# A selective scan's backward direction: two of its sixteen input products move to ScalarE and TensorE

## The chip, the cores and the metric

The kernel runs on one core of one Trainium2 chip. The metric is the device time of one execution in microseconds (us). Lower is better.

## The reference, cut to what matters

The whole network is an attention layer, a recurrent layer, a Mamba layer and a mixture of experts over 16384 tokens of 64 channels. The change touches the Mamba layer alone, which runs once over the tokens as they stand and once over them reversed:

```python
dt = jax.nn.softplus(dt @ dt_w.T + dt_b)
A = -jnp.exp(A_log)
dA = jnp.exp(dt[..., None] * A)
dBx = dt[..., None] * Bm[:, :, None, :] * xc[..., None]

def step(h, inp):
    dA_t, dBx_t, C_t = inp
    h = dA_t * h + dBx_t
    y = jnp.einsum('bds,bs->bd', h, C_t)
    return (h, y)
...
y = jnp.swapaxes(ys, 0, 1) + xc * D
y = y * jax.nn.silu(z)
return y @ out_w.T
...
y_bwd = jnp.flip(_mamba(jnp.flip(x_flat, axis=1), *params), axis=1)
return (y_fwd + y_bwd).reshape(Bn, Hn, Wn, C)
```

There are 128 inner channels and 16 states. `xc` is the SiLU of a causal convolution with four taps; `Bm`, `Cm` and the raw `dt` are linear in `xc`.

## The kernel before, in words

Stages run one after the other on all engines: attention, recurrence, normalization, the scan (`state_scan`), experts. The scan keeps the 128 inner channels on the partitions and takes the tokens in 16 blocks of 1024 for each direction, `NC = 16`, forward first. Inside a block it takes the 16 states in turn, s = 0 to 15; below, such a turn is called unit s.

For each state and block the following happens, each on a tile of 128 x 1024:

- **The decay**, exp(dt A[s]), is made by ScalarE: into the SBUF ring `dA` (`decay_v`) or into the PSUM buffer `p_u[s % 2]` (`decay_g`).
- **The input product**, dt x times B's row s, comes about in one of three ways. *By VectorE* (`BY_VECTOR`): TensorE spreads B's row over all partitions into `p_u[s % 2]` (`spread_b` of TensorE) and VectorE multiplies in place (`inject` of VectorE); the decay is then in SBUF. *By GpSimd* (the states in neither table): SP loads the row spread over all partitions, 512 KB, into the ring `bb`, and GpSimd multiplies into `dbx` (`inject` of GpSimd); the decay is then in `p_u[s % 2]`. *By ScalarE and TensorE's turns* (`BY_SCALAR`): dt x stands transposed in `dtxT`, tokens on the partitions, so that B is a scale per partition; ScalarE makes eight scaled copies of 128 x 128 (`scale`), and TensorE turns these back into `p_u[s % 2]` (`turn_in`); the decay is in SBUF.
- **The scan**, by VectorE (`tensor_tensor_scan`, in `unit`), reads decay and input and writes the ring `h`.
- **The read**, by GpSimd (`read_c`), multiplies `h` by C's row into the ring `hc`, and TensorE adds it up over the states in `p_y` (`total`), four units later (`LAG_SUM`).

Before, the forward direction has eight states by VectorE, four by ScalarE (3, 5, 9, 12) and four by GpSimd; backward has ten by VectorE, none by ScalarE and six by GpSimd (2, 5, 7, 10, 13, 15).

While a block is scanned, the next one is prepared through one PSUM buffer, `p_p`, which passes from step to step: the convolution (TensorE, units 0 and 1), its SiLU (`silu_x`, ScalarE, unit 1), the rows of B and C (`in_out`, TensorE, units 2 and 3), their copy and store (`bc_rows`, ScalarE, unit 4), backward the gate's input (`gate_in`, unit 4, and `take_z`, unit 5), the step size (`step_size`, unit 6), its softplus (ScalarE, VectorE and GpSimd's `linear_and_log`, units 7 to 11) and dt x (`dt_x`, VectorE, unit 12). Where states go by ScalarE, B's columns (`columns_b`, `take_columns_b`) and the turned dt x (`turn_x`, `take_turned_x`) pass through it too. Backward, the block before is finished as well: the gate (VectorE, behind unit 3's scan), which waits for the last of the 16 sums, the projection (`project`, TensorE) and its addition to `x` (`add_x`, VectorE).

The order is written out by hand. `run` calls each engine's `unit` for s = 0 to 15 and behind it the steps that the engine's tables `prepare`, `tail` and `own` name for this s. Every engine works strictly in its order and waits on semaphores. In `unit`, each engine works ahead by a number of states:

```python
C_RING, B_RING, TURN_RING = 4, 2, 2
DECAY_AHEAD, INJECT_AHEAD, SCALE_AHEAD, LAG_SUM = 3, 2, 3, 4
```

So ScalarE issues state 4's decay and scalings in unit 1, and TensorE issues state 4's spreading or turn in unit 3, ahead of the sum that is due in that unit. A `p_u` buffer comes free for state s when the scan of state s - 2 is done.

## Time and profile before

| | |
|---|---|
| median of 3 runs | 2569.32 us (2566.36 to 2575.73) |
| the profiled execution | 2567.49 us, span 2565.7 us |
| busy: TensorE, VectorE, ScalarE, GpSimd | 2189.9, 2180.1, 1763.6, 2076.0 us |
| forward scan | about 650 to 1488 us |
| backward scan | about 1488 to 2363 us |

Busy times are sums of instruction durations. TensorE's are partly modelled, and neighbouring instructions of VectorE, ScalarE and GpSimd overlap by up to 0.1 us, so that the start-to-start distance in the timeline is the better measure of what one costs. "Idle before" names who ended an engine's idle time.

### The profile page before, as it was taken

The page shows a single profiled execution, that of the slowest core. Times are in us where ns is not written, and L with a number is a line of the kernel's source. Part 1 is how long each engine was busy: PE and PEld are TensorE (multiplying, and loading weights), DVE is VectorE, ACT ScalarE, POOL GpSimd, SP SyncE. Part 2 cuts the span into 40 slices and gives each one's busy share as a digit, 9 for nine tenths or more (in the row PEclk, how much of TensorE's full clock was granted, in tenths as well). Part 3 has the DMA queues.
Part 4 walks back from the last instruction along what each step waited for, and adds up shares of the span by engine and source line. Part 5 has one row for each costly group of instructions (what it writes and reads, how often), then busy time and mean ns, then how long its engine had stood idle before and what let it go on. Part 6 is the DMA issues. An engine that isn't in the chain of part 4 may idle for free. (4 is left out here: it accounts for less than half of the span.)

```text
span 2565.7 us, 37339 instructions
## 1 busy us (share of the span) xinstructions
PE 2189.9 (85%) x9229; PEld 1137.4 (44%) x9306; DVE 2180.1 (85%) x2229; ACT 1763.6 (69%) x3998; POOL 2076.0 (81%) x1330
## 2 busy tenths in 40 slices
PE   8899997774799888998899888899889898887597
PEld 8566665562344444444444433343333333333543
DVE  5577777434899999999999999999999999997766
ACT  4799997565788877887788855656556565553386
POOL 4355555203899999999999999999999999997389
PEclk7899998786899999999999999999999999999799
DMA  3000000003677676676667777777777777773032
GB/s 70 13 12 12 12 11 9 1 1 85 222 228 231 219 232 225 231 230 226 227 226 235 228 240 253 244 231 239 239 234 248 233 244 237 230 245 127 3 69 60
DMA packets 192553, 421.10 MB, mean 164 GB/s; under 512 B 66548, under 2 KB 95705, under 8 KB 192474
## 3 DMA queue, kind: packets, MB, share of 16 engines
q1 hardware_dynamic: 190938, 416.01, 51.6%
q10 hardware_dynamic: 1536, 4.20, 0.5%
q8 instruction: 30, 0.49, 0.1%
q14 instruction: 49, 0.40, 0.1%
HBM read 387.63 MB, written 24.12 MB: 160 GB/s over the span
## 5 line engine op out<-in xcount | busy, mean ns | idle before, releaser
L1574 POOL TENSOR_TENSOR s_hc<-s_h,s_cc 128x1024 f32<-128x1024 f32 x512 | 1202.6, 2370 | 51.0 <-PE s_py L1337 37.3
L1337 PE MATMUL s_py<-s_hc,ident 128*128 128x512 f32 x2048 | 979.3, 603 | 19.1 <-DVE s_yo L1620 19.1
L1657 DVE TENSOR_TENSOR_SCAN s_h<-s_dA,s_state,s_pu 128x1024 f32<-128x1024 f32 x330 | 770.3, 2342 | 27.7 <-PE s_pu L1315 4.7
L1337 PEld LDWEIGHTS s_py<-s_hc,ident 128*128 128x128 f32 x2048 | 385.9, 193 | 384.7 <-issue 312.0
L1490 ACT ACTIVATE s_dA<-s_dt,ss_A 128x1024 f32<-128x1024 f32 x352 | 401.6, 1142 | 9.1 <-ACT s_brow L1453 7.7
L1495 ACT ACTIVATE s_pu<-s_dt,ss_A 128x1024 f32<-128x1024 f32 x160 | 178.4, 1115 | 322.0 <-DVE s_h L1657 316.8
L1567 POOL TENSOR_TENSOR s_dbx<-s_dtx,s_bb 128x1024 f32<-128x1024 f32 x160 | 379.1, 2369 | 6.9 <-DMA s_bb<-rows_scratch 6.9
L1657 DVE TENSOR_TENSOR_SCAN s_h<-s_pu,s_state,s_dbx 128x1024 f32<-128x1024 f32 x150 | 350.2, 2335 | 22.3 <-ACT s_pu L1495 20.1
L1633 DVE TENSOR_TENSOR s_pu<-s_pu,s_dtx 128x1024 f32<-128x1024 f32 x288 | 349.0, 1212 | 14.9 <-PE s_pu L1324 12.5
L1324 PE MATMUL s_pu<-s_bcs,ss_sel 128*128 128x512 bf16 x499 | 159.6, 390 | 133.8 <-DVE s_h L1657 129.7
L591 POOL TENSOR_TENSOR ar_ex<-ar_ex,ar_rs 128x512 f32<-128x512 f32 x128 | 133.3, 1041 | 157.8 <-DVE ar_rs L540 157.7
L629 ACT ACTIVATE ar_ex<-ar_sc,ar_mn 128x128 f32<-128x128 f32 x512 | 199.2, 391 | 5.5 <-DVE ar_mn L535 3.0
L1324 PEld LDWEIGHTS s_pu<-s_bcs,ss_sel 128*128 128x128 bf16 x576 | 42.1, 98 | 323.6 <-DVE s_h L1657 224.5
L1473 ACT ACTIVATE s_sT<-s_dtxT,s_bT 128x128 f32<-128x128 f32 x512 | 156.4, 388 | 0.2
L1925 PE MATMUL ee_ps<-ex_we,ex_xg 128*128 128x512 f32 x256 | 113.9, 606 | 30.2 <-DMA ex_xg<-ex_xT 30.2
L1270 PE MATMUL s_pp<-s_n,ss_taps 128*128 128x512 f32 x256 | 122.3, 601 | 10.3 <-DMA s_n<-n_scratch 10.3
L531 DVE TENSOR_TENSOR ar_sc<-ar_pss,at_bias 128x512 f32<-128x512 f32 x128 | 88.6, 692 | 18.3 <-PE ar_pss L475 15.5
L1943 ACT ACTIVATE ee_hw<-ee_ps,ex_wt 128x64 f32<-128x64 f32 x384 | 92.2, 317 | 15.7 <-PE ee_ps L1925 6.4
L1982 POOL TENSOR_TENSOR ee_hw<-ee_hw 128x1024 f32<-128x1024 f32 x32 | 75.4, 2355 | 33.6 <-DVE ee_hw L1951 33.6
L553 DVE SCALAR_TENSOR_TENSOR x_tok<-ar_pso,at_maskT,x_tok 128x64 f32 (+1 forms) x128 | 36.2, 283 | 76.8 <-POOL x_tok L586 70.7
L1502 ACT COPY s_state<-s_h 128x1 f32<-128x1 f32 x510 | 86.9, 180 | 18.5 <-DVE s_h L1657 17.9
L629 ACT ACTIVATION_READ_ACCUMULATOR ar_ex<-ar_sc,ar_mn 128x1 f32 x512 | 96.3, 188 | 0.0
(272 smaller groups left out, 3590.3 us busy)
## 6 DMA issues: line engine op xcount, KB each, us to landing
s_cc<-rows_scratch SPq DMA_DIRECT2D x512, 512.0 KB, 4.6
s_bb<-rows_scratch SPq DMA_DIRECT2D x160, 512.0 KB, 5.0
s_n<-n_scratch SPq DMA_DIRECT2D x64, 258.0 KB, 5.5
y_scratch<-s_yo SPq DMA_DIRECT2D x16, 512.0 KB, 5.4
s_yf<-y_scratch SPq DMA_DIRECT2D x16, 512.0 KB, 6.6
x_tok<-in_x_dram SPq DMA_DIRECT2D x16, 256.0 KB, 4.5
at_xg<-at_xT SPq DMA_DIRECT2D x64, 64.0 KB, 2.1
n_scratch<-ss_turned SPq DMA_DIRECT2D x32, 128.0 KB, 2.8
```

The source lines that it names most:

```text
L591: nc.gpsimd.tensor_tensor(ex[:, j, :, :], ex[:, j, :, :], by_head, ALU.mult).then_inc(evened, 1)
L629: ins = nc.scalar.activation(ex[:, j, h, :], sc[:, j, h, :], ACT.Exp, bias=mn[:, j, h:h + 1], scale=-1.0, accum_out=tot[:, j, h:h + 1])
L1270: ins = nc.tensor.matmul(p_p[:, hf], lhsT=k["taps"][:, int(w.back), pair, :], rhs=ns[:, par, at:at + HALF], start=(pair == 0), stop=(pair ...
L1324: ins = nc.tensor.matmul(p_u[s % 2][:, hf], lhsT=k["sel"][:, s:s + 1].to_broadcast([128, 128]), rhs=bcs[:, par, hf], start=True, stop=True)
L1337: ins = nc.tensor.matmul(p_y[:, hf], lhsT=c.ident[:, :], rhs=hc[:, s % RING, hf], start=(s == 0), stop=(s == U - 1))
L1473: ins = nc.scalar.activation(sT[:, r % TURN_RING, j, :], dtxT[:, j, :], ACT.Copy, scale=bT[:, par, j, s:s + 1])
L1490: nc.scalar.activation(dA[:, w.d.index(s) % w.decay_ring, :], dt[:, par, :], ACT.Exp, scale=k["A"][:, s:s + 1]).then_inc(v_decayed, 1)
L1495: nc.scalar.activation(p_u[s % 2][:, :], dt[:, par, :], ACT.Exp, scale=k["A"][:, s:s + 1]).then_inc(g_decayed, 1)
L1567: nc.gpsimd.tensor_tensor(dbx[:, r % B_RING, :], dtx[:, par, :], bb[:, r % B_RING, :], ALU.mult).then_inc(g_injected, 1)
L1574: nc.gpsimd.tensor_tensor(hc[:, s % RING, :], h[:, s % RING, :], cc[:, s % C_RING, :], ALU.mult).then_inc(read, 1)
L1633: nc.vector.tensor_tensor(p_u[s % 2][:, :], p_u[s % 2][:, :], dtx[:, par, :], ALU.mult).then_inc(v_injected, 1)
L1657: nc.vector.tensor_tensor_scan(out=flow(h[:, s % RING, :]), data0=flow(decays), data1=flow(inputs), initial=begun, op0=ALU.mult, op1=ALU.a ...
```

## The change

Backward, states 4 and 10 go by ScalarE and TensorE's turns, nine states (0, 1, 3, 6, 7, 9, 12, 13, 15) by VectorE and five (2, 5, 8, 11, 14) by GpSimd. Backward blocks therefore also make B's columns (unit 5 on TensorE, 6 on ScalarE) and the turned dt x (units 13 and 14). The projection moves from unit 13 to unit 14 and waits for the turned dt x to be copied, its addition from unit 14 to 15. The step size waits for the copied columns, the columns wait for the copied gate input. The ring of decays has four buffers (five before). The waits on B's ring count for five products in two slots: `spreads` counts the loads of one slot, and SP's `spread_b` waits, at the first rows of a block, for the last user of that slot in the block before. Forward blocks are as before.

```diff
 BY_VECTOR = ((0, 1, 4, 7, 8, 11, 13, 15),
-             (0, 1, 3, 4, 6, 8, 9, 11, 12, 14))
-BY_SCALAR = ((3, 5, 9, 12), ())
+             (0, 1, 3, 6, 7, 9, 12, 13, 15))
+BY_SCALAR = ((3, 5, 9, 12), (4, 10))
...
-        self.decay_ring = 4 if len(self.d) % 4 == 0 else 5
+        self.decay_ring = 5 if len(self.d) % 5 == 0 else 4
...
+    def spreads(self, n, slot):
+
+        w = self.of(n)
+        per = len(range(slot, len(w.g), B_RING))
+        done = NC * len(range(slot, len(w.before.g), B_RING)) if w.before is not None else 0
+        return n * per + (done - w.start * per)
...
             def step_size(hf):
                 def step(w, m, par):
-                    bc_taken(w, m)
-                    if w.back:
-                        need(pe, z_copied, m - NC)
+                    pe.wait_ge(bt_taken, m + 1)
...
             def columns_b(w, m, par):
                 pe.wait_ge(r_copied, m + 1)
+                if w.back:
+                    need(pe, z_copied, m - NC)
...
             def project(w, m, par):
-                pe.wait_ge(dtx_done, end(m + 3, ALL))
+                pe.wait_ge(xt_taken, end(m + 3, ALL))
...
-                backward: shared + [(5, step_size(a)), (6, step_size(b))]}
-            tail = {forward: (), backward: [(13, project)]}
+                backward: shared + [(5, columns_b), (6, step_size(a)), (6, step_size(b)), (13, turn_x)]}
+            tail = {forward: (), backward: [(14, project)]}
...
-                       backward: first + rest_of}
+                       backward: first + [(6, take_columns_b)] + rest_of + [(14, take_turned_x)]}
...
-            tail = {forward: (), backward: [(LAG_SUM - 1, gate), (14, add_x)]}
+            tail = {forward: (), backward: [(LAG_SUM - 1, gate), (15, add_x)]}
...
                 r = w.g.index(s)
                 if r == 0:
                     sp.wait_ge(r_stored, 16 * (n + 1))
-                need(sp, g_injected, w.upto(G, n) + r + 1 - B_RING)
+                if r >= B_RING:
+                    sp.wait_ge(g_injected, w.upto(G, n) + r - B_RING + 1)
+                elif n:
+                    last = range(r, len(way_of(n - 1).g), B_RING)[-1]
+                    sp.wait_ge(g_injected, w.upto(G, n) - len(way_of(n - 1).g) + last + 1)
```

Three places of the order follow, each in a late backward block. Line numbers are those of either kernel; behind the first tables they differ by one.

**ScalarE, units 1 to 4**, from the decay of state 4 (the first `s_dA`) on; `s_state` is the copy of a scan's last column, `s_brow` that of the rows of B and C. Before:

```order
L1490 ACTIVATE s_dA<-s_dt,ss_A 128x1024
L1502 COPY s_state<-s_h 128x1
L1409 ACT_TABLE_LOAD
L1409 ACTIVATE s_xc<-s_pp,ss_cb 128x1024
L1415 ACTIVATE s_zs<-s_zs 128x1024
L1418 ACT_TABLE_LOAD
L1502 COPY s_state<-s_h 128x1
L1490 ACTIVATE s_dA<-s_dt,ss_A 128x1024
L1502 COPY s_state<-s_h 128x1
L1495 ACTIVATE s_pu<-s_dt,ss_A 128x1024
L1502 COPY s_state<-s_h 128x1
L1453 COPY s_brow<-s_pp 32x1024
```

Now, from the same decay:

```order
L1489 ACTIVATE s_dA<-s_dt,ss_A 128x1024
L1501 COPY s_state<-s_h 128x1
L1472 ACTIVATE s_sT<-s_dtxT,s_bT 128x128 x8
L1408 ACT_TABLE_LOAD
L1408 ACTIVATE s_xc<-s_pp,ss_cb 128x1024
L1414 ACTIVATE s_zs<-s_zs 128x1024
L1417 ACT_TABLE_LOAD
L1501 COPY s_state<-s_h 128x1
L1489 ACTIVATE s_dA<-s_dt,ss_A 128x1024
L1501 COPY s_state<-s_h 128x1
L1494 ACTIVATE s_pu<-s_dt,ss_A 128x1024
L1489 ACTIVATE s_dA<-s_dt,ss_A 128x1024
```

The eight scalings of state 4 stand between its decay and the table load of the convolution's SiLU (`s_xc`), and the decay of state 7, the last row, is ahead of the copy of the rows, which follows it.

**TensorE, units 1 to 5**, from the second half of the convolution (`ss_taps`) on; `s_py` are the sums, `s_pu` from `s_bcs` a spreading, `ss_wbc` into 32 rows the rows of B and C, `ss_wz` the gate's input. Before:

```order
L1270 MATMUL s_pp<-s_n,ss_taps 128x512 x2
L1324 MATMUL s_pu<-s_bcs,ss_sel 128x512 x2
L1337 MATMUL s_py<-s_hc,ident 128x512 x2
L1289 MATMUL s_pp<-s_xc,ss_wbc 32x512
L1324 MATMUL s_pu<-s_bcs,ss_sel 128x512 x2
L1337 MATMUL s_py<-s_hc,ident 128x512 x2
L1289 MATMUL s_pp<-s_xc,ss_wbc 32x512
L1337 MATMUL s_py<-s_hc,ident 128x512 x2
L1253 MATMUL s_pp<-s_n,ss_wz 128x512 x2
L1324 MATMUL s_pu<-s_bcs,ss_sel 128x512 x2
```

Now:

```order
L1269 MATMUL s_pp<-s_n,ss_taps 128x512 x2
L1323 MATMUL s_pu<-s_bcs,ss_sel 128x512 x2
L1336 MATMUL s_py<-s_hc,ident 128x512 x2
L1286 MATMUL s_pp<-s_xc,ss_wbc 32x512
L1314 MATMUL s_pu<-ident,s_sT 128x128 x8
L1336 MATMUL s_py<-s_hc,ident 128x512 x2
L1286 MATMUL s_pp<-s_xc,ss_wbc 32x512
L1336 MATMUL s_py<-s_hc,ident 128x512 x2
L1255 MATMUL s_pp<-s_n,ss_wz 128x512 x2
L1323 MATMUL s_pu<-s_bcs,ss_sel 128x512 x2
L1336 MATMUL s_py<-s_hc,ident 128x512 x2
L1297 MATMUL s_pp<-ss_wbc,s_xc 128x16 x8
```

State 4's turn (`s_pu` from `s_sT`) stands where its spreading stood, behind the first half of the rows of B and C and ahead of the block's last sum. State 5 goes by GpSimd as before, and B's columns (128x16) come behind state 6's spreading and a sum.

**GpSimd, units 6 to 10**, with its reads (`s_hc`), its products (`s_dbx`) and its sum for the step size (`s_tc`). Before:

```order
L1574 TENSOR_TENSOR s_hc<-s_h,s_cc 128x1024 x3
L1567 TENSOR_TENSOR s_dbx<-s_dtx,s_bb 128x1024
L1574 TENSOR_TENSOR s_hc<-s_h,s_cc 128x1024
L1554 TENSOR_TENSOR s_rest<-s_flat,s_parts 128x128
L1574 TENSOR_TENSOR s_hc<-s_h,s_cc 128x1024
L1548 TENSOR_TENSOR s_tc<-s_tc,s_tb 128x1024
L1574 TENSOR_TENSOR s_hc<-s_h,s_cc 128x1024
```

Now:

```order
L1573 TENSOR_TENSOR s_hc<-s_h,s_cc 128x1024 x3
L1553 TENSOR_TENSOR s_rest<-s_flat,s_parts 128x128
L1566 TENSOR_TENSOR s_dbx<-s_dtx,s_bb 128x1024
L1573 TENSOR_TENSOR s_hc<-s_h,s_cc 128x1024
L1547 TENSOR_TENSOR s_tc<-s_tc,s_tb 128x1024
L1573 TENSOR_TENSOR s_hc<-s_h,s_cc 128x1024
```

A product, state 11's, now stands between the rest of B's rows (`s_rest`) and the sum for the step size.

## Rows read from the trace of the kernel before

**Rows 1.** Windows view; forward scan, backward scan from first to 15th gate, one backward block
```profile
core 0: us, PE busy (x) PEld busy (x) DVE busy (x) ACT busy (x) POOL busy (x), PEclk, DMA share, GB/s
675.00:1481.00 806.00, 722.73 (x2341) 342.81 (x2378) 763.27 (x418) 639.39 (x1231) 765.84 (x358) 1.00 0.70 229
1554.00:2314.50 760.50, 671.06 (x1747) 287.35 (x1780) 745.56 (x435) 445.75 (x644) 757.75 (x351) 0.97 0.74 239
2206.03:2260.23 54.20, 47.08 (x126) 19.98 (x128) 53.17 (x32) 31.95 (x47) 53.98 (x26) 1.00 0.73 238
```

**Rows 2.** Groups of instructions, VectorE, forward scan, 675 to 1481 us
```profile
L1657 DVE TENSOR_TENSOR_SCAN s_h<-s_dA,s_state,s_pu 128x1024 f32<-128x1024 f32 x179 | 416.1, 2339 | 14.6 <-PE s_pu L1315 4.7
L1633 DVE TENSOR_TENSOR s_pu<-s_pu,s_dtx 128x1024 f32<-128x1024 f32 x123 | 149.5, 1216 | 6.8 <-PE s_pu L1324 5.6
L1657 DVE TENSOR_TENSOR_SCAN s_h<-s_pu,s_state,s_dbx 128x1024 f32<-128x1024 f32 x60 | 140.2, 2337 | 21.2 <-ACT s_pu L1495 19.3 <-POOL s_hc L1574 1.6
```

**Rows 3.** Timeline, VectorE, a backward block: scans, products, gate, step-size sum
```profile
2193.26 2.35 DVE L1657 TENSOR_TENSOR_SCAN s_h<-s_dA,s_state,s_pu 128x1024 f32<-128x1024 f32 x1
...
2201.35 1.21 DVE L1633 TENSOR_TENSOR s_pu<-s_pu,s_dtx 128x1024 f32<-128x1024 f32 x1
2202.66 2.35 DVE L1657 TENSOR_TENSOR_SCAN s_h<-s_dA,s_state,s_pu 128x1024 f32<-128x1024 f32 x1
2204.92 1.21 DVE L1633 TENSOR_TENSOR s_pu<-s_pu,s_dtx 128x1024 f32<-128x1024 f32 x1
2206.03 1.22 DVE L1620 TENSOR_TENSOR s_yo<-s_py,s_zs 128x1024 f32<-128x1024 f32 x1
...
2229.32 1.22 DVE L1606 TENSOR_TENSOR s_pp<-s_tc,s_pp 128x1024 f32<-128x1024 f32 x1
```

**Rows 4.** Timeline, ScalarE, the same block
```profile
2195.65 1.12 ACT L1495 ACTIVATE s_pu<-s_dt,ss_A 128x1024 f32<-128x1024 f32 x1 [6.22 <-DVE s_h L1657]
...
2197.93 1.28 ACT L1409 ACT_TABLE_LOAD   x1
2199.61 1.11 ACT L1409 ACTIVATE s_xc<-s_pp,ss_cb 128x1024 f32<-128x1024 f32 x1 [0.39 <-PE s_pp L1270]
```

**Rows 5.** Timeline, TensorE, the same block
```profile
2201.65 1.04 PE L1289 MATMUL s_pp<-s_xc,ss_wbc 128*32 128x512 f32 x2
2202.62 0.61 PE L1324 MATMUL s_pu<-s_bcs,ss_sel 128*128 128x512 bf16 x2
2203.07 1.88 PE L1337 MATMUL s_py<-s_hc,ident 128*128 128x512 f32 x4
...
2207.38 1.98 PE L1337 MATMUL s_py<-s_hc,ident 128*128 128x512 f32 x4 [1.46 <-DVE s_yo L1620]
```

**Rows 6.** Timeline, forward block (GpSimd, ScalarE, TensorE, VectorE), then GpSimd backward
```profile
1048.76 2.38 POOL L1548 TENSOR_TENSOR s_tc<-s_tc,s_tb 128x1024 f32<-128x1024 f32 x1
...
1101.96 2.37 POOL L1548 TENSOR_TENSOR s_tc<-s_tc,s_tb 128x1024 f32<-128x1024 f32 x1
...
1064.63 2.44 ACT L1473 ACTIVATE s_sT<-s_dtxT,s_bT 128x128 f32<-128x128 f32 x8
...
1075.32 1.03 PE L1315 MATMUL s_pu<-ident,s_sT 128*128 128x128 f32 x8
...
1086.06 1.96 PE L1298 MATMUL s_pp<-ss_wbc,s_xc 128*128 128x16 f32 x16
...
1087.85 2.35 DVE L1657 TENSOR_TENSOR_SCAN s_h<-s_pu,s_state,s_dbx 128x1024 f32<-128x1024 f32 x1 [1.31 <-ACT s_pu L1495]
...
2183.49 2.39 POOL L1567 TENSOR_TENSOR s_dbx<-s_dtx,s_bb 128x1024 f32<-128x1024 f32 x1
...
2225.90 2.37 POOL L1548 TENSOR_TENSOR s_tc<-s_tc,s_tb 128x1024 f32<-128x1024 f32 x1
```

**Rows 7.** Page, part 6: issues by SP, KB each, us to landing
```profile
s_bb<-rows_scratch SPq DMA_DIRECT2D x160, 512.0 KB, 5.0
```

More of the change, by code:

```diff
@@ L1151, in state_scan @@
     V, A, DEC, G = (lambda w: w.v), (lambda w: w.a), (lambda w: w.d), (lambda w: w.g)
-    assert forward.a and not backward.a
     with ExitStack() as ctx:
@@ L1240, in _ @@
         def _(pe):
-            def bc_taken(w, m):
-                pe.wait_ge(*((bt_taken, m + 1) if w is forward else (r_copied, m + 1)))
             def gate_in(hf):
@@ L1251, in step @@
                     if last:
-                        pe.wait_ge(dtx_done, ALL)
+                        pe.wait_ge(xt_taken, ALL)
                     ins = nc.tensor.matmul(p_p[:, hf], lhsT=k["z"][:, :],
@@ L1261, in step @@
                     pe.wait_ge(n_loaded[par], 16 * (m + 2 - par))
-                    if w is forward or (isinstance(m, int) and m == NC):
-                        need(pe, xt_taken, m)
-                    else:
-                        pe.wait_ge(dtx_done, m)
+                    need(pe, xt_taken, m)
                     if w.back:
@@ L1564, in inject @@
                     pool.wait_ge(dtx_done, n + 1)
-                pool.wait_ge(b_spread[r % B_RING], 16 * (w.upto(G, n, B_RING) + r // B_RING + 1))
+                pool.wait_ge(b_spread[r % B_RING], 16 * (w.spreads(n, r % B_RING) + r // B_RING + 1))
                 need(pool, scanned, w.past(G, n, s, lambda v: B_RING))
```

## The prediction, made before the changed kernel ran

> **What bounds the kernel now.** The windows view comes first [rows 1]. From the first backward gate to the 15th, 14 blocks of 54.3 us, GpSimd is busy 757.75 us of 760.5 and VectorE 745.56. In one block (1024 tokens, 16 states), gate to gate, GpSimd has 53.98 of 54.20 us, VectorE 53.17, ScalarE 31.95, TensorE 47.08. The first two are a double limit: relief must reach both. VectorE's instructions overlap a little, so their starts in the timeline count [rows 3]: 2.26 us from a scan to the next instruction (2202.66 to 2204.92), 1.31 from a product to its own scan (2201.35 to 2202.66), 1.11 from a product to other work (2204.92 to 2206.03). It hardly waits. TensorE is the engine to watch: 47 us of work, and an order written by hand in which one late step holds up all behind it. ScalarE has room in sum, but works in bursts.
>
> The forward scan already uses the method that the change brings backward, for four states of sixteen. Its work is less (eight products by VectorE, four by GpSimd), yet a block takes 53.20 us (1048.76 to 1101.96) [rows 6], and VectorE waits 14.6 + 6.8 + 21.2 us over some 15 blocks, 2.8 us each, the named part for TensorE's spreadings and turns and for ScalarE's decays [rows 2]. That is the warning: the method makes waits that sums don't show.
>
> **The change, part by part**, for one backward block; times t count from the start of state 0's scan, 2193.26 [rows 3].
>
> *GpSimd* loses one product: 2.39 us less an overlap of 0.07, 2.3 [rows 6]; 53.98 becomes 51.7. *VectorE* loses one: 54.2 - 1.3 = 52.9. Every state still has one decay by ScalarE. *SP* loses one load of 512 KB. With five products in a ring of two, the next block's first row of B goes into the slot of this block's last (state 14), so SP now waits for that product before it issues. GpSimd has four reads, 9 us, before it needs the row, against 5.0 us to landing [rows 7]. Queued behind this wait on SP is a row of C of the same size, late by one product; it has three reads, 7 us. Cost: nothing, or 0.5 us a block if this cover is too thin. The decay ring of four still lets ScalarE work three states ahead; nothing.
>
> *ScalarE* gets two rounds of eight scalings (2.44 us less the overlap, 2.35 each) [rows 6], a copy of the turned input, about 1.0 as the SiLU of that shape [rows 4], and a short one of B's columns, 0.3 estimated from the scalings: 31.95 + 6.0 = 38 us. *TensorE* gets two turns (1.03 less the overlap, 0.87 each), the turned input (eight such transposes again, 0.9) and B's columns (1.96, so 1.8), and loses one spreading (0.45, 2202.62 to 2203.07) [rows 5, 6]: 47.1 + 4.0 = 51 of 53 us. Its 7.1 us of idle time (54.20 - 47.08) take them in, if the order lets it.
>
> *The projection, one state later.* The copy of the turned input stands behind the decay that scan 13 releases and is done 2.2 us after scan 13; the projection (sixteen small matmuls, like B's columns, 1.8) is done at 4.1. VectorE adds it only after scan 14, a product, scan 15 and a product, 7 us. State 0's spreading, queued behind the projection, is due at 5.8. Cost nothing; were the copy over 1 us late, that spreading would be next.
>
> *The first wait, at the gate.* State 4's scalings stand on ScalarE between state 4's decay and the convolution's SiLU (the order rows of the change). ScalarE starts the decay of state 2 at t = 2.39, since that waits for scan 0; its table load begins at 4.67 and the SiLU at 6.35, after 0.39 us for the convolution [rows 4]. With 2.35 us in front, the load begins at 7.02, the SiLU at 8.31 and is done at 9.4. TensorE reaches the first half of B's and C's rows at 8.39 [rows 5] and now waits until 9.45. Then follow, in its order, that half (0.97), state 4's turn (0.87) and the last sum of the block before (1.88 less the overlap, 1.81): 13.10. The gate needs that sum. Before, it was done at 11.62 and the gate started at 12.77, 1.15 us of slack. Now state 4 has no product on VectorE, 1.11 us less, so the gate is due at 11.66: **a wait of 1.4 us**. Were the SiLU not late at all, 8.39 + 0.97 + 0.87 + 1.81 = 12.04 would still leave 0.4. The saved product is paid back where it was saved.
>
> A rule bears on this place. ScalarE's table load takes 1.28 us, and the SiLU behind it starts 0.40 us later, of which 0.39 are put down to the convolution [rows 4]. The Trainium skill, ScalarE: Activation LUTs, What ACT_TABLE_LOAD costs, adds a drain of about 1.38 us to each switch, 2.66 us in all. By that the gate would wait 2.8 us and the time would be 2598. The row shows no such drain; this way keeps a chance of 0.02, inside the slower case.
>
> *The second wait, state 7's spreading.* The gate ends at 14.2. TensorE's sum for state 0 (1.98 less the overlap) ends at 16.2, when ScalarE has also copied B's and C's rows; the gate's input (as long) at 18.2; state 6's spreading, a sum and B's columns, which are new, at 22.15; state 7's spreading at 22.75. VectorE wants it at 22.3: 0.45 us [rows 5, 6]. It is the small difference of two long chains; I take 0.1, bounds 0 and 0.45. The step size, which now waits for the copy of B's columns, finds it done.
>
> *The third, the sum for the step size.* State 11's product now stands ahead of it on GpSimd. From the read of state 4 at 16.6: read, product 8, read 5, read 6, read 7 (from 26.35), the rest (0.4), product 11, read 8 and the sum (2.3 each) end at 36.0; VectorE wants it at 35.5. Today it is 1 us early (2225.90 + 2.37 against 2229.32) [rows 3, 6]. I take 0.3, bounds 0 and 0.6.
>
> **The sum.** 54.2 - 1.3 + 1.4 + 0.1 + 0.3 = 54.7 us a block, 0.5 more; 16 blocks give +8 us on the profiled execution's 2567.49, so 2575.5, **2576 us**. That execution lies 1.8 us below the median shown, 2569.32; the forecast is 0.3% above that median, **no change that can be told**: a measurement of this kernel tells about 0.5%, 12.8 us, or 0.8 us a block. With the waits at their lower bounds (0.4, 0, 0) the block takes 53.3 and the time is 2553; with the upper (1.7, 0.45, 0.6) and 0.5 for SP it takes 56.15, 2599.
>
> **Rivals.**
> *Faster (0.25): VectorE's own sum decides.* For it: GpSimd is behind today, and with it TensorE's sums; once it follows the scans, TensorE may run earlier and the gate's path shrink. Against it: that path starts at scan 0 and runs through ScalarE, not GpSimd. 52.9 to 53.3 us a block, 2547 to 2553; I name 2548. The Trainium skill, Perfetto Trace Analysis, Identifying the Most-Contended Engine, judges by occupancy; by that the block falls to VectorE's 52.9 us and this case is the forecast. The forward block speaks against it: its fullest engine, GpSimd, is busy 765.84 of 806 us, 95% [rows 1], and VectorE waits its 2.8 us all the same.
>
> *Slower (0.30): TensorE has no slack left.* With 51 us of work in 53 every late spreading, turn or sum becomes VectorE's wait, in the first nine states above all; in the forward block state 6 alone waits 1.31 us [rows 6]. It decides once the waits pass 2.1 us a block (1.3 + 0.8). With the forward block's 2.8 in place of my 1.8 it is 55.7, 2592; with 0.6 more, for a TensorE that is fuller here, 2601. I name 2593. For it: forward TensorE is busy 722.73 of 806 us, 90% [rows 1], here it would be 96%. Against it: two scaled states, not four, and far apart.
>
> *The clock.* TensorE's granted clock averages 0.97 backward, so it falls to 1.2 GHz from 2.4 now and then; it is 1.00 forward and in the block chosen [rows 1]. Backward TensorE idles 7.1 us of a block, forward 5.5. With less idle time here the falls should go: the mean block (54.3) would come to the undisturbed one (54.2), minus 2 us in all. A fall in the first half of a block would lengthen the path to the gate instead; part of the slower case.
>
> That the change doesn't do what it says is ruled out by the order rows: eight turns where a spreading was, B's columns, and the new order on GpSimd.
>
> **Chances.** The likeliest case, waits that give the saving back, 0.45, centre 2576. Faster by over 0.5% (below 2556.5): 0.25. Slower by over 0.5% (above 2582.2): 0.30, from the upper end of my case and its rival. Within: 0.45. For 8 in 10 the range runs from 2549, just above the faster case's centre, to 2597, between the slower case's 2593 and 2601.
>
> **What would show it.** After: 54.7 us gate to gate; the gate waits over 1 us for TensorE's sum; GpSimd idles 2 to 3 us a block; the SiLU starts near t = 8.3; VectorE waits 0 to 0.6 us for GpSimd's sum; B's loads number 144, not 160. Wrong if the gate doesn't wait (then 2548), or if VectorE waits over 2.1 us a block for spreadings, turns and decays (then 2593).

## The result: 44 us slower, and the profile after

| | before | changed |
|---|---|---|
| median of four runs each, us | 2569.75 | 2613.72 |
| range, us | 2566.36 to 2575.73 | 2612.57 to 2622.89 |
| profiled execution, us | 2567.49 | 2622.89 |
| backward, gate to gate, median of 15 blocks in the profile, us | 54.27 | 57.08 |
| of it from the gate to the step size's sum | 23.33 | 24.67 |
| of it from that sum to the next gate | 30.83 | 32.45 |

The ratio is 1.0176, interval 1.0147 to 1.0206: slower, outside the forecast range of 2549 to 2597. The profiled execution of the changed kernel is the slowest of its four, 9 us above the median; its first scan starts at 657.73 us, before the change at 649.97, so part of the difference between the two profiled executions lies in stages that the change doesn't touch. The 44 us of the medians are 2.8 us for each of sixteen backward blocks, which is what the median block shows. The last two rows of the table are differences of VectorE's starts in the timeline, medians too, and are used below for every kernel. They are formed one by one and need not add up exactly.

Windows view after, backward from 1554 us as in [rows 1], and one block, gate to gate:

```profile
1554.00:2314.50 760.50, 684.00 (x2151) 326.91 (x2190) 690.35 (x396) 501.56 (x851) 687.80 (x318) 0.98 0.66 217
2199.41:2256.86 57.45, 52.18 (x164) 24.97 (x166) 52.38 (x30) 37.70 (x65) 52.00 (x24) 0.97 0.67 217
```

The work is what was added up: VectorE 52.38 us a block (forecast 52.9 with the gaps between instructions), GpSimd 52.00 (51.7), ScalarE 37.70 (38), TensorE 52.18 (51). No engine is full. GpSimd, which had 0.2 us to spare in a block, now idles 5.45 (2 to 3 were forecast), and the time is in waits. The waits of VectorE, then those of GpSimd, 1554 to 2360 us (total, times, longest), and last GpSimd's in the same stretch before the change:

```profile
DVE s_pp L1605 <- POOL s_tc L1547: 29.8, 14, 2.2
DVE s_yo L1619 <- PE s_py L1336: 24.6, 14, 2.1
DVE s_pu L1632 <- PE s_pu L1323: 7.3, 19, 1.6
```

```profile
POOL s_hc L1573 <- PE s_py L1336: 46.7, 49, 2.0
POOL s_hc L1573 <- DVE s_h L1656: 31.2, 33, 1.6
```

```profile
POOL s_hc L1574 <- PE s_py L1337: 4.1, 9, 1.6
```

In the block below VectorE waits 1.67 us at the gate, forecast 1.4, and 2.14 us for the step size's sum, where 0.3 was forecast. GpSimd waits for TensorE's sums 46.7 us in place of 4.1. Timeline of the block: VectorE's scan of state 0, the gate, state 7's product and scan, the step size's sum and the next block's first product; then ScalarE, TensorE and GpSimd:

```profile
2186.02 2.34 DVE L1656 TENSOR_TENSOR_SCAN s_h<-s_dA,s_state,s_pu 128x1024 f32<-128x1024 f32 x1
...
2199.41 1.23 DVE L1619 TENSOR_TENSOR s_yo<-s_py,s_zs 128x1024 f32<-128x1024 f32 x1 [1.67 <-PE s_py L1336]
...
2209.08 1.23 DVE L1632 TENSOR_TENSOR s_pu<-s_pu,s_dtx 128x1024 f32<-128x1024 f32 x1 [0.16 <-PE s_pu L1323]
2210.41 2.35 DVE L1656 TENSOR_TENSOR_SCAN s_h<-s_dA,s_state,s_pu 128x1024 f32<-128x1024 f32 x1
...
2224.09 1.23 DVE L1605 TENSOR_TENSOR s_pp<-s_tc,s_pp 128x1024 f32<-128x1024 f32 x1 [2.14 <-POOL s_tc L1547]
...
2241.76 1.23 DVE L1632 TENSOR_TENSOR s_pu<-s_pu,s_dtx 128x1024 f32<-128x1024 f32 x1 [0.30 <-PE s_pu L1323]
```

```profile
2190.56 2.44 ACT L1472 ACTIVATE s_sT<-s_dtxT,s_bT 128x128 f32<-128x128 f32 x8
2193.02 1.28 ACT L1408 ACT_TABLE_LOAD   x1
2194.32 1.11 ACT L1408 ACTIVATE s_xc<-s_pp,ss_cb 128x1024 f32<-128x1024 f32 x1
```

```profile
2206.74 1.85 PE L1297 MATMUL s_pp<-ss_wbc,s_xc 128*128 128x16 f32 x16
...
2208.88 1.88 PE L1336 MATMUL s_py<-s_hc,ident 128*128 128x512 f32 x4
2210.59 1.88 PE L1278 MATMUL s_pp<-s_xc,ss_wdt 128*128 128x512 f32 x4
2212.31 1.88 PE L1336 MATMUL s_py<-s_hc,ident 128*128 128x512 f32 x4
...
2233.45 1.10 PE L1305 MATMUL s_pp<-ident,s_dtx 128*128 128x128 f32 x8 [1.78 <-DVE s_dtx L1611]
2235.70 1.04 PE L1323 MATMUL s_pu<-s_bcs,ss_sel 128*128 128x512 bf16 x2 [1.16 <-DVE s_h L1656]
2236.53 3.03 PE L1336 MATMUL s_py<-s_hc,ident 128*128 128x512 f32 x4
```

```profile
2202.97 2.35 POOL L1573 TENSOR_TENSOR s_hc<-s_h,s_cc 128x1024 f32<-128x1024 f32 x1 [1.18 <-DVE s_h L1656]
...
2210.90 2.36 POOL L1573 TENSOR_TENSOR s_hc<-s_h,s_cc 128x1024 f32<-128x1024 f32 x1 [0.95 <-PE s_py L1336]
2214.34 2.36 POOL L1573 TENSOR_TENSOR s_hc<-s_h,s_cc 128x1024 f32<-128x1024 f32 x1 [1.08 <-PE s_py L1336]
2216.66 0.43 POOL L1553 TENSOR_TENSOR s_rest<-s_flat,s_parts 128x128 f32<-128x128 f32 x1
2217.05 2.38 POOL L1566 TENSOR_TENSOR s_dbx<-s_dtx,s_bb 128x1024 f32<-128x1024 f32 x1
2219.37 2.38 POOL L1573 TENSOR_TENSOR s_hc<-s_h,s_cc 128x1024 f32<-128x1024 f32 x1
2221.70 2.35 POOL L1547 TENSOR_TENSOR s_tc<-s_tc,s_tb 128x1024 f32<-128x1024 f32 x1
```

Read them against each other. TensorE's sum for state 2 ends at 2208.88 + 1.88 = 2210.76, and GpSimd's read of state 6, which needs that buffer of the ring of four, starts at 2210.90 after 0.95 us of waiting. The sum for state 3 ends at 2214.19, read 7 starts at 2214.34 after 1.08. From there GpSimd runs without a gap: rest, state 11's product, read 8, the step size's sum, done at 2224.05; VectorE goes on at 2224.09. The two waits of GpSimd are 2.03 us. Not all of that is TensorE's: read 7 also needs scan 7, which ends at 2210.41 + 2.35 = 2212.76, so without any wait for TensorE it would start some 1.5 us sooner than 2214.34. The other 0.6 us of VectorE's 2.14 is GpSimd's own order, in which state 11's product stands ahead of the sum.

### The profile page after: what moved, and what is told of

The parts are those of the page before. It is cut to its first block and busy times, and to the rows that moved or that the text cites. A ratio compares the mean times of both kernels' runs of the same rounds, so it can differ in the third digit from the quotient of the medians.

```text
span 2620.9 us, 38848 instructions
## 1 busy us (share of the span) xinstructions
PE 2253.7 (86%) x9827; PEld 1209.7 (46%) x9914; DVE 2166.4 (83%) x2213; ACT 1855.6 (71%) x4286; POOL 2041.5 (78%) x1314
## 5 line engine op out<-in xcount | busy, mean ns | idle before, releaser
L1656 DVE TENSOR_TENSOR_SCAN s_h<-s_dA,s_state,s_pu 128x1024 f32<-128x1024 f32 x345 | 805.1, 2341 | 26.6 <-PE s_pu L1314 4.7
L1489 ACT ACTIVATE s_dA<-s_dt,ss_A 128x1024 f32<-128x1024 f32 x368 | 419.8, 1142 | 88.7 <-DVE s_h L1656 87.3
L1632 DVE TENSOR_TENSOR s_pu<-s_pu,s_dtx 128x1024 f32<-128x1024 f32 x272 | 330.5, 1215 | 24.4 <-PE s_pu L1323 21.8
L1566 POOL TENSOR_TENSOR s_dbx<-s_dtx,s_bb 128x1024 f32<-128x1024 f32 x144 | 340.2, 2363 | 6.3 <-DMA s_bb<-rows_scratch 6.3
L1656 DVE TENSOR_TENSOR_SCAN s_h<-s_pu,s_state,s_dbx 128x1024 f32<-128x1024 f32 x135 | 314.8, 2332 | 19.8 <-ACT s_pu L1494 17.6
L1494 ACT ACTIVATE s_pu<-s_dt,ss_A 128x1024 f32<-128x1024 f32 x144 | 160.5, 1114 | 231.2 <-DVE s_h L1656 225.2
L1323 PE MATMUL s_pu<-s_bcs,ss_sel 128*128 128x512 bf16 x457 | 148.0, 391 | 103.8 <-DVE s_h L1656 99.5
L1472 ACT ACTIVATE s_sT<-s_dtxT,s_bT 128x128 f32<-128x128 f32 x768 | 234.7, 389 | 0.2
L1314 PEld LDWEIGHTS s_pu<-ident,s_sT 128*128 128x128 f32 x768 | 86.1, 141 | 91.2 <-issue 73.7
L1314 PE MATMUL s_pu<-ident,s_sT 128*128 128x128 f32 x768 | 102.5, 277 | 24.0 <-ACT s_sT L1472 21.5
L531 DVE TENSOR_TENSOR ar_sc<-ar_pss,at_bias 128x512 f32<-128x512 f32 x128 | 88.5, 692 | 18.2 <-PE ar_pss L475 15.5
```

Source lines behind the costliest of these rows:

```text
L1314: ins = nc.tensor.transpose(p_u[s % 2][:, j * Q:(j + 1) * Q], sT[:, r % TURN_RING, j, :], c.ident[:, :])
L1323: ins = nc.tensor.matmul(p_u[s % 2][:, hf], lhsT=k["sel"][:, s:s + 1].to_broadcast([128, 128]), rhs=bcs[:, par, hf], start=True, stop=True)
L1472: ins = nc.scalar.activation(sT[:, r % TURN_RING, j, :], dtxT[:, j, :], ACT.Copy, scale=bT[:, par, j, s:s + 1])
L1489: nc.scalar.activation(dA[:, w.d.index(s) % w.decay_ring, :], dt[:, par, :], ACT.Exp, scale=k["A"][:, s:s + 1]).then_inc(v_decayed, 1)
L1494: nc.scalar.activation(p_u[s % 2][:, :], dt[:, par, :], ACT.Exp, scale=k["A"][:, s:s + 1]).then_inc(g_decayed, 1)
L1566: nc.gpsimd.tensor_tensor(dbx[:, r % B_RING, :], dtx[:, par, :], bb[:, r % B_RING, :], ALU.mult).then_inc(g_injected, 1)
```

## The experiments

Times are medians; the ratio is to the kernel before, run on the same chip beside it, as recorded; it is not the quotient of two medians. The kernel before had medians of 2569.7 to 2572.9 us in these sets of runs, so differences of a few microseconds between rows are not told: number 3 lies 34 us below the change by the medians and 1.55%, 40 us, by the ratios. "Gate to sum" and "sum to gate" are the two parts of a backward block.

| kernel | us | ratio (interval) | gate to sum | sum to gate |
|---|---|---|---|---|
| the change | 2613.7 | 1.0176 (1.0147 to 1.0206) | 24.67 | 32.45 |
| 1 sum before turn | 2612.4 | 1.016 (1.0143 to 1.0177) | 24.98 | 31.72 |
| 2 SiLU first | 2627.6 | 1.0226 (1.0206 to 1.0245) | 27.30 | 30.77 |
| 3 step size's sum ahead | 2579.3 | 1.0021 (1.0007 to 1.0035) | 22.46 | 32.37 |
| 4 no B columns | 2594.5 | 1.0088 (1.0068 to 1.0109) | 22.98 | 32.40 |
| 6 rows behind sum | 2624.2 | 1.0195 (1.0174 to 1.0216) | 27.51 | 30.65 |
| 7 = 6 and 3 | 2573.3 | 1.0005 (0.9992 to 1.0019) | 23.59 | 31.26 |
| 8 projection only | 2564.7 | 0.9977 (0.9966 to 0.9987) | 23.46 | 30.62 |
| 9 scaling early | 2606.1 | 1.0121 (1.0099 to 1.0144) | 24.67 | 31.79 |
| 10 = 9 and 3 | 2569.7 | 0.9988 (0.9973 to 1.0003) | 22.45 | 31.84 |
| 11 = 9, 3 and 6 | 2564.5 | 0.9960 (0.9945 to 0.9975) | 22.76 | 30.68 |
| 12 before, 8 scalings more | 2574.3 | 1.0009 (0.9994 to 1.0024) | 23.30 | 30.95 |
| 13 B columns later | 2625.8 | 1.0211 (1.0193 to 1.0228) | 25.29 | 32.39 |
| 14 = 11, spreading ahead | 2568.7 | 0.9995 (0.9977 to 1.0012) | 22.95 | 31.55 |

**1. The last sum ahead of state 4's turn on TensorE** (backward, unit 3).

```diff
-                if mw is not None and ms in mw.a:
+                late = w.back and s == 3
+                if mw is not None and ms in mw.a and not late:
                     turn_in(mw, m, mpar, ms)
...
+                if late:
+                    turn_in(mw, m, mpar, ms)
```

> TensorE computes the last sum of the block before ahead of state 4's turn, backward; nothing else changes. Theory A (the gate waits for one chain: SiLU, first half of B's and C's rows, turn, sum): the sum comes one turn (about 0.9 us) sooner, the gate's wait falls from 1.67 us to 0.7 to 0.8, and the block gets about 0.9 us shorter, 14 us in all: about 2600. The wait for the step size's sum stays at 2.1, because the chain from the gate through TensorE's sums to GpSimd moves with the gate. Theory B (the engines have no slack, a wait taken away comes back elsewhere): the sum of the waits per block stays near 4.3 us and the time stays at 2612 to 2616.

The gate's wait halves, as theory A says (in one block 0.81 us). Most of the gain of 14 us does not come: 2612.4 is 1 us below the change by the medians, 4 by the ratios. In the trace the blocks are 0.5 us shorter, and the stretch from the first scan to the last gate is 12 us shorter than in the change's trace, but one execution of each doesn't settle a size that the four of each don't show. Where a part of it goes can be read: state 6's spreading, for which nothing waited in the change, is now 0.40 us late in nearly every block. The waits of VectorE:

```profile
DVE s_pp L1608 <- POOL s_tc L1550: 29.9, 14, 2.2
DVE s_yo L1622 <- PE s_py L1336: 13.7, 15, 1.2
DVE s_pu L1635 <- PE s_pu L1323: 9.0, 29, 0.5
```

**2. State 4's scalings behind both SiLUs** (with the edit of 1).

```diff
-                if mw is not None and ms in mw.a:
+                if mw is not None and ms in mw.a and not (mw.back and ms == 4):
                     scale(mw, m, mpar, ms)
...
-            own = {forward: tables, backward: tables + [(5, take_z)]}
+            own = {forward: tables, backward: [(1, scale_4)] + tables + [(5, take_z)]}
```

> As the one before, and ScalarE computes state 4's eight scalings behind the two SiLUs and not ahead of them. Theory A: the SiLU starts when the convolution is done, about 2 us sooner, the gate's wait is gone (0 to 0.3 us), the block is about 1.7 us shorter than with the change, 55.7, and the time about 2588; the wait for the step size's sum stays at 2.1. Theory B: the time falls by less than 6 us from 2613, because state 4's turn or a spreading becomes late instead.

Theory A falls as a forecast of time. The gate waits 3.0 us in all in place of 24.6, yet the time rises by 14 us. The wait is now at state 6's spreading (34.3 us for spreadings over 28 products against 7.3 over 19). ScalarE's copy of B's and C's rows starts 15.39 us after scan 0 in every second block and 16.88 in most of the others (15.07 in the change), because ScalarE works up to it without a gap: loads, SiLUs, scalings and decays. TensorE's gate input and the spreading behind it wait for that copy. In one block TensorE has finished the rows at 2205.70, ScalarE copies them at 2208.21, and TensorE's gate input waits 1.65 us for that.

**3. The step size's sum directly behind state 11's product on GpSimd.**

```diff
                     inject(mw, m, mpar, ms)
+                if nxt is not None and nxt.back and s == 9:
+                    linear_and_log(nxt, n + 1, 1 - par)
                 if s:
                     read_c(n, s - 1)
...
-            prepare = [(8, part_rest), (9, linear_and_log), (10, part_low)]
+            prepare = {forward: [(8, part_rest), (9, linear_and_log), (10, part_low)],
+                       backward: [(8, part_rest), (10, part_low)]}
```

> GpSimd adds the two parts of the step size directly behind the product for state 11, ahead of the read of state 8; nothing else changes. Theory C (the wait of 2.1 us is only a place in GpSimd's order): the sum is ready 2.3 us sooner, the wait vanishes, the gate's wait stays at 1.7, and the time falls by about 2.2 us a block, to about 2579. Theory B: the read of state 8 is late in its place, TensorE's sums and the spreadings behind them slip, and less than half of that comes back: above 2596.

2579.3 against the 2579 of theory C. One instruction moved by one place on GpSimd gives back 34 of the 44 us. VectorE's waits:

```profile
DVE s_yo L1622 <- PE s_py L1336: 24.9, 15, 2.1
DVE s_pu L1635 <- PE s_pu L1323: 3.2, 15, 0.5
```

The read of state 8 now comes behind the sum, and no new wait of VectorE follows from it. The gate waits as before.

**4. B's columns left out backward** (TensorE's sixteen small matmuls and ScalarE's copy). This kernel leaves out that part of the computation: the scaled states use the forward scan's last columns.

```diff
-                backward: shared + [(5, columns_b), (6, step_size(a)), ...
+                backward: shared + [(6, step_size(a)), ...
...
-                       backward: first + [(6, take_columns_b)] + rest_of + ...
+                       backward: first + rest_of + ...
```

> Backward, TensorE leaves out B's columns (sixteen small matmuls, 1.85 us) and ScalarE their copy (0.27 us), so the scaled states use the forward scan's last columns; this part of the computation is left out. Theory D (the wait for the step size's sum comes from TensorE: the late gate and the new columns delay its sums 2 and 3, whose buffers GpSimd's reads 6 and 7 wait for, 0.95 and 1.08 us): the two waits of GpSimd fall to 0 and 0 to 0.2, the wait for the sum from 2.14 to 0.2 to 0.4, the gate's stays at 1.7, and the time is about 2584. Theory E (GpSimd's own order, with state 11's product ahead of the sum, makes the wait): it stays above 1.5 us and the time falls by less than 10 us.

Between the theories, nearer to D: GpSimd's waits for TensorE's sums fall from 46.7 us to 18.2, VectorE's wait for the step size's sum from 2.14 to 0.71, the time by 19 us. So the new work on TensorE reaches VectorE by way of GpSimd, and the columns alone are 1.4 us of the 2.14. The 0.71 that stay are GpSimd's own order with state 11's product in it, of which E spoke. D's size (29 us) was too large.

**6. Both halves of B's and C's rows behind the last sum.** (There is no number 5.)

```diff
-                backward: shared + [(5, columns_b), ...
+                backward: shared[:2] + [(3, in_out(a)), (3, in_out(b)), (5, columns_b), ...
```

> Backward, TensorE computes both halves of B's and C's rows behind the last sum of the block before, in place of the first half two places ahead of it; nothing else changes. Theory A (the gate waits because the product that needs the late SiLU stands ahead of its sum): the sum no longer waits for the SiLU, the gate's wait of 1.65 us is gone (0 to 0.1), and no spreading becomes late, because both halves are still done by the time the second half is done now. Theory F (what binds is the stretch from the gate through TensorE's sums to the step size's sum, which moves with the gate): the wait for the step size's sum stays at 2.1 us and the time falls by 1.7 us a block, to about 2586. Theory B (the waits come back elsewhere, as with the scalings behind the SiLU): above 2604.

The gate's wait is gone, and the kernel is 10 us slower than the change: theory B's side, with two reasons that can be read. ScalarE, then TensorE behind the gate (at 2198.74 here):

```profile
2202.17 1.00 ACT L1453 COPY s_brow<-s_pp 32x1024 f32<-32x1024 f32 x1
```

```profile
2203.22 1.98 PE L1255 MATMUL s_pp<-s_n,ss_wz 64*128 64x512 f32 x4 [1.17 <-ACT s_brow L1453]
2205.14 0.95 PE L1323 MATMUL s_pu<-s_bcs,ss_sel 128*128 128x512 bf16 x2
2205.88 3.27 PE L1336 MATMUL s_py<-s_hc,ident 128*128 128x512 f32 x4
```

ScalarE copies the rows 15.08 us after scan 0; in the changed kernel it is 15.07 (2201.09 less 2186.02). The gate comes sooner, and the gate's input must wait for ScalarE, whose burst of scalings, two table loads, SiLUs and decays ends no sooner. That is the first reason. The second is the clock: behind the gate's input the next sum takes 3.27 us and not 1.88. Windows view of number 6, the same stretch behind the second gate and behind this one; the granted clock, third from the end, is 1.00 and 0.55, so most of the second ran at 1.2 GHz:

```profile
1627.37:1631.17 3.80, 3.80 (x23) 2.75 (x22) 3.21 (x2) 2.14 (x3) 3.45 (x2) 1.00 0.62 222
2205.20:2209.00 3.80, 3.80 (x8) 1.71 (x8) 2.77 (x2) 2.14 (x3) 1.91 (x1) 0.55 0.68 268
```

The granted clock is 0.55 to 0.61 there in eight of the fourteen blocks to 2325 us and 1.00 in six. Seven of the eight take 58.2 us, with state 7's spreading 1.1 to 1.7 us late; the three that have no slowed sum anywhere take 56.45, less than the 57.05 of such blocks of the change. So where the clock holds, number 6 gains 0.6 us a block, and by these blocks it is the clock that turns this into a loss; no run changes the clock alone.

**7. Numbers 6 and 3 together.**

> The one before together with the step size's addition directly behind state 11's product on GpSimd. If the two waits are two independent places in two orders, both are gone, the block falls to VectorE's own 52.9 us with 0.2 to 0.6 of small waits, and the time is 2549 to 2557: faster than before the change by 0.6 to 0.9%. If TensorE, busy 51 of 53 us, then binds, its waits come back as spreadings that VectorE waits for, over 1 us a block, and the time is 2565 or more.

2573.3: the second case. With the sum moved and the gate free, the spreadings wait, 20.1 us over 33 products (to 2300 us), state 6's 0.9 to 1.3 us in each block.

**8. The kernel before with the projection one state later.**

```diff
-            tail = {forward: (), backward: [(13, project)]}
+            tail = {forward: (), backward: [(14, project)]}
-            tail = {forward: (), backward: [(LAG_SUM - 1, gate), (14, add_x)]}
+            tail = {forward: (), backward: [(LAG_SUM - 1, gate), (15, add_x)]}
```

> The kernel before with the change's projection alone: TensorE's projection and VectorE's addition of it one state later, the products as before. By the prediction this costs nothing: within 0.2% of before, 2565 to 2575. If the later projection is what delays the convolution of the next block and with it the SiLU, the gate waits over 0.5 us and the time is over 2580.

At the lower edge of what was expected: 2564.7, ratio 0.9977, an interval that leaves out 1. It is no cost, rather a gain of 6 us: in the profile the mean block, from the first gate to the last, is 53.40 us against 53.68, 4 us over the fifteen blocks. Why is not shown.

**9. State 4's scalings behind the copy of the turned input, a block ahead, in ScalarE's idle time.**

```diff
-                if mw is not None and ms in mw.a:
+                if mw is not None and ms in mw.a and not (mw.back and ms == 4):
                     scale(mw, m, mpar, ms)
...
-                       backward: first + [(6, take_columns_b)] + rest_of + [(14, take_turned_x)]}
+                       backward: first + [(6, take_columns_b)] + rest_of + [(14, take_turned_x), (14, scale_4)]}
```

> Backward, ScalarE scales for state 4 of the next block directly behind the copy of the turned input, where it idles 3.6 us, and no longer between scan 0 and the SiLU; nothing else changes. Theory H (the crowded stretch is ScalarE's: scalings, load, two SiLUs, load, three decays, the copy of B's and C's rows, for which TensorE's gate input waits): the copy of the rows comes about 1 us sooner against scan 0, the gate's wait falls to 0.4, no spreading is late, and the time falls by 15 to 20 us to 2594 to 2600; the wait for the step size's sum stays near 2.1, as it moves with the gate. Theory F alone (only the stretch behind the gate binds, and what comes ahead of it is free): above 2606, as when the sum was put ahead of the turn.

8 us less than the change by the medians, at the edge of theory F and short of H's 14 to 20. "Gate to sum" stays at 24.67 to the hundredth. In the block shown the SiLU comes only 0.6 us sooner, because the table load itself waits for the convolution. ScalarE here (scan 0 at 2169.84), and in a block of number 11 where it does not:

```profile
2176.24 1.28 ACT L1408 ACT_TABLE_LOAD   x1 [1.76 <-PE s_pp L1269]
2177.54 1.11 ACT L1408 ACTIVATE s_xc<-s_pp,ss_cb 128x1024 f32<-128x1024 f32 x1
```

```profile
2194.79 1.28 ACT L1409 ACT_TABLE_LOAD   x1
2197.24 1.11 ACT L1409 ACTIVATE s_xc<-s_pp,ss_cb 128x1024 f32<-128x1024 f32 x1 [1.16 <-PE s_pp L1269]
```

**10. Numbers 9 and 3 together.**

> The one before together with the step size's addition directly behind state 11's product on GpSimd. Theory H: the gate's wait 0.4 us, no spreading waits over 0.2 us as there were with the rows behind the sum, the block 53.4 to 53.8 us, and the time 2556 to 2564. If TensorE's work binds in itself, spreadings wait 1 us a block and the time is 2570 or more.

2569.7, 6 us above the upper end of what H gave: no spreading waits over 0.2 us, but the gate still waits, 0.7 to 1.3 us in the blocks whose table load starts at once and 1.4 to 1.8 in those whose table load waits for the convolution, turn about.

**11. Numbers 9, 3 and 6 together.**

> The one before with both halves of B's and C's rows behind the last sum of the block before. Theory H: the gate no longer waits; the rows' second half is done no later than before, so the block comes to 53.1 to 53.4 us and the time to 2550 to 2557. If the first half's place matters to the copy of the rows, the gate's 0.4 us comes back as a late spreading and it equals the one before.

2564.5, ratio 0.9960: below the kernel before, and the best of these. It misses its range (2550 to 2557). What is left, to 2300 us:

```profile
DVE s_pu L1637 <- PE s_pu L1323: 11.7, 27, 1.2
DVE s_yo L1624 <- PE s_py L1336: 1.3, 3, 0.7
```

The miss can be located. Counted from the first gate, state 6's spreading is 0.2 to 0.4 us late in the odd blocks and, from the fourth to the twelfth, 1.1 to 1.2 in the even ones. In those even blocks the table load waits for the convolution, and the copy of the rows starts 14.9 to 15.5 us after scan 0; in the odd ones it starts at 13.9 to 14.0. The blocks take 54.1 to 54.5 us in the first case and, where no sum is slowed, 53.2 to 53.4 in the second, which is what was expected of all; half of the blocks at 0.9 us more are 7 us. ScalarE in the twelfth block (scan 0 at 2135.80), then VectorE's product for state 6:

```profile
2142.85 1.28 ACT L1409 ACT_TABLE_LOAD   x1 [2.41 <-PE s_pp L1269]
2144.15 1.11 ACT L1409 ACTIVATE s_xc<-s_pp,ss_cb 128x1024 f32<-128x1024 f32 x1
...
2150.92 1.00 ACT L1453 COPY s_brow<-s_pp 32x1024 f32<-32x1024 f32 x1
```

```profile
2154.53 1.23 DVE L1637 TENSOR_TENSOR s_pu<-s_pu,s_dtx 128x1024 f32<-128x1024 f32 x1 [1.24 <-PE s_pu L1323]
```

No run moves the load alone, so this is read from the traces and not shown by a change.

Number 8 alone has 0.9977. The medians are equal, 2564.5 and 2564.7, and the intervals overlap. So what number 11 gains over the kernel before is no more than the later projection may give by itself; that the products taken from VectorE and GpSimd add anything is not shown.

**12. The kernel before with eight scalings more ahead of the SiLU** (their result is not used).

```diff
+                if w.back and s == 1:
+                    act.wait_ge(turned_in, NC * len(forward.a))
+                    for j in range(BLOCKS):
+                        nc.scalar.activation(sT[:, 0, j, :], dtxT[:, j, :], ACT.Copy, scale=bT[:, 0, j, 4:5])
```

> The kernel before, with eight scalings more on ScalarE in every backward block, ahead of the SiLU, where the change puts state 4's; their result is not used. It prices ScalarE's 2.35 us by itself: the SiLU starts about 2 us later, the first half of the rows about 1 us, and the gate just in time. Theory A and H (it costs only what passes the slack of 1.15 us at the gate): 0 to 0.4 us a block, 2570 to 2577. If every microsecond ahead of the SiLU is on the path already: 2 us a block, 2600.

As expected, 2574.3: ScalarE's 2.35 us cost nothing that can be told while they meet slack.

**13. B's columns behind state 7's spreading and the sum for state 2.**

```diff
-                backward: shared + [(5, columns_b), (6, step_size(a)), ...
+                backward: shared + [(6, columns_b), (6, step_size(a)), ...
```

> The changed kernel with B's columns one place later on TensorE, behind state 7's spreading and the sum for state 2 and still ahead of the step size's products; nothing else changes. Theory J (one chain: TensorE from the gate through its sums, then GpSimd's reads to the step size's sum; a wait on it only changes its place): state 7's spreading comes 1.8 us sooner and is not waited for, but the sum for state 3, which releases GpSimd's read 7, stays where it is, so the wait for the step size's sum becomes 2.3 to 2.4 us and the time stays at 2610 to 2617. Theory A (each wait has its own cause; the sum waits because TensorE is behind): TensorE is relieved at state 7, the total of the waits falls by 1 us a block or more, and the time is below 2600.

No gain but 12 us more: one chain, as J has it, and longer. VectorE's waits to 2300 us:

```profile
DVE s_yo L1619 <- PE s_py L1336: 22.5, 13, 2.1
DVE s_pp L1605 <- POOL s_tc L1547: 15.9, 13, 1.3
DVE s_pp L1599 <- ACT s_ta L1436: 13.6, 13, 1.1
DVE s_pu L1632 <- PE s_pu L1323: 11.4, 18, 1.7
```

J had the wait stay in one place at 2.3 to 2.4; it is spread over three (1.22 for the sum, 1.04 for ScalarE's softplus, 0.55 for a spreading, in one block). What J says of the chain holds: the start of the sum for state 3 is 12.90 us behind the gate in the change (2212.31 less 2199.41) and 13.52 here (2216.77 less 2203.25), since the step size's products must wait for ScalarE's copy of the columns; and from there to the step size's sum it is 11.78 us in both (2224.09 less 2212.31, 2228.55 less 2216.77). The 0.62 us are those by which "gate to sum" grew.

**14. Number 11 with state 6's spreading ahead of the gate's input.**

```diff
-                if mw is not None and ms in mw.v:
+                if mw is not None and ms in mw.v and not (mw.back and ms == 6):
                     spread_b(mw, m, mpar, ms)
...
-                   backward: [(4, gate_in(a)), (4, gate_in(b))] + add
+                   backward: [(4, spread_6), (4, gate_in(a)), (4, gate_in(b))] + add
```

> The best so far (state 4's scalings in ScalarE's idle time, the step size's addition ahead of a read, B's and C's rows behind the sum) with state 6's spreading ahead of the gate's input on TensorE. Its wait of 0.4 us goes and everything behind moves 0.45 us later, where state 7's spreading is already waited for 0.17 us. If that one takes it all, it becomes 0.3 to 0.6 us and the time stays at 2561 to 2567; if the order was the cause, the block loses 0.3 us and the time is 2557 to 2561.

2568.7, a little above its upper case and above number 11: state 7's spreading, now 0.84 us late in one block and 1.17 in the next, in turn, takes more than was freed.

## Why the prediction was wrong

**The engines' sums: right.** All four came within 1.2 us. *VectorE's own block*: 57.45 less the four waits shown (1.67, 0.16, 2.14, 0.30) is 53.18; each wait also costs the 0.1 us by which unwaited instructions overlap, which leaves 52.8 against 52.9.

**The gate: right.** 1.67 us against 1.4, inside its bounds. The SiLU starts 8.30 us after scan 0 (2194.32 less 2186.02), forecast 8.31. *The table load without a drain: right.* The load ends at 2194.30 and the SiLU starts at 2194.32; the 1.38 us that the Trainium skill, ScalarE: Activation LUTs, What ACT_TABLE_LOAD costs, adds are not there.

**State 7's spreading: right**, 0.16 us against 0.1, with some luck: the worked chain said 0.45, and the 0.1 was a choice.

**The third wait: wrong, and this is the step that failed.** The prediction strung GpSimd's instructions from read 4 to the step size's sum together by their durations, let read 7 wait for its scan (26.35), but none of them for TensorE, and came to 36.0 us, due at 35.5. Read 4 did begin at 16.95 (2202.97), forecast 16.6. Read 7 began at 28.32 (2214.34), 2.0 us behind the forecast, and the sum was done 38.0 us after scan 0 (2224.05), 2.0 behind its own. Between stand the waits of reads 6 and 7 for TensorE's sums 2 and 3. The prediction had put B's columns into TensorE's order as far as state 7's spreading, 0.1 us, and there it stopped; the delay runs on through sum 2, the step size's products and sum 3, and comes back to GpSimd through the four buffers of its reads. Before the change that edge stood at 4.1 us over the same stretch of the backward scan, so it was there to be seen, with little time on it. The upper bound of 0.6 was therefore no bound.

Number 4 gives the columns' share: without them the wait is 0.71 us, near the 0.5 by which the prediction's own chain came out late. The late gate is no part of it: in number 1 its wait halves, in number 6 it is gone, and this wait stays at 2.13. Both ends hang on the gate. Number 3 gives the price: with this wait alone removed the kernel takes 2579.3, against a forecast of 2576 that held 5 us for it.

**The rivals.** The slower case had the right sign, and its point (waits past 2.1 us a block) was passed by the sum of all waits, 4.3 us. By the sign that was set for it, spreadings, turns and decays that VectorE waits for, it was not: they are 7.3 us in all, 0.5 a block. TensorE's order is what binds, but by way of GpSimd, and it gave 2593, not 2614. "No slack left" is too strong as well: number 3 gives 34 us back and relieves TensorE of nothing. The faster case fell. *Occupancy* says no more here than before: at 52 of 57 us no engine looks like the limit.

**The clock.** The falls did not go: the granted clock averages 0.98 after, 0.97 before [rows 1]. Blocks of the change without a slowed sum take 57.05 us, and the mean of the fourteen is 57.57, so what goes with the falls is about 0.5 us a block, where the forecast had 2 us less in all. That is about 7 us, on a trace that is itself 9 us slow. In the block shown TensorE idles around the turned input, then the granted clock is 0.58 (windows view below), the sum in that stretch takes 3.03 us in place of 1.88, and the next block's first product waits 0.30 for a spreading behind it.

```profile
2235.70:2239.40 3.70, 3.70 (x7) 1.67 (x8) 3.60 (x3) 2.20 (x4) 2.62 (x2) 0.58 0.98 302
```

**The edits with no cost: right.** VectorE and GpSimd wait for no row of B in the backward part of the waits view, so SP's new wait costs nothing. 144 loads of B are issued. The projection costs nothing and may give 6 us.

**One chain or several waits.** From one gate to the step size's sum VectorE needs 22.45 us (numbers 3 and 10); the path gate, TensorE's sums and B's columns, GpSimd's reads and product needs 24.67. What comes sooner ahead of the gate therefore lets the gate start sooner only as long as the second limit, ScalarE's burst up to the copy of the rows, follows. Numbers 2 and 6 took the gate's wait away without shortening that burst: 2 lengthened it and lost, 6 left it and won only in the blocks where the clock held; 9 shortened it a little and won a little. Both have to be relieved together, as in number 11. Open stays why the table load waits in every second block, and how many of TensorE's clock falls a version has: to 2300 us number 11's trace shows 1.00 where number 14's shows 0.97, and no run changed the clock alone.

## What to carry to other kernels

When work is moved in kernels whose engines run fixed orders, follow a late instruction through every ring buffer until it meets slack: a buffer that is released without a wait today is an edge with little time on it, not an edge that is absent. Before removing the largest wait, ask which path fixes the distance to the next one; two waits that hang on one path are paid once, and an instruction placed one slot earlier on the engine that ends the path (34 us here) can be worth more than the work that was saved (21 us at best).

## What the runs showed of the hardware that was not expected

The table load ahead of the SiLU does not always go ahead. Before the change 13 loads in the backward scan (1554 to 2360 us) idled 12.5 us and their SiLUs 3.3 us: in one block the load starts at once and the SiLU waits for the convolution, as in [rows 4], in the next the load waits and the SiLU comes 1.30 us behind it, turn about in all but the last. Numbers 9, 10, 11 and 14 alternate in the same way; it is about what number 11, and part of what number 10, lost against the expectation. The change hides it: with the scalings in front, its 14 loads idle 1.4 us in all. The groups view of the kernel before:

```profile
L1409 ACT ACT_TABLE_LOAD x13 | 16.7, 1283 | 12.5 <-PE s_pp L1270 12.4
L1409 ACT ACTIVATE s_xc<-s_pp,ss_cb 128x1024 f32<-128x1024 f32 x13 | 14.5, 1114 | 3.3 <-PE s_pp L1270 3.2
```

Where a block has the second form, scalings of 2.35 us ahead of the load cover a wait that was there anyway, and number 12 may be cheap for that reason too.

A short idle time of TensorE may cost twice, but not each time: in number 6 a wait of 1.17 us stands ahead of a stretch at 0.55 to 0.61 of the clock in eight blocks, in which one sum takes 1.0 to 1.5 us more than its like, and the same wait stands ahead of a stretch at 1.00 in three.
